# Five small bias loads on ScalarE's DMA queue, issued after adj has landed instead of at once

## What is computed

```python
def _L0_gnn_ref(x, in_mat, out_mat, w3_w, w3_b, u3_w, u3_b, w4_w, w4_b, w5_w, w5_b, u5_w, u5_b):
    h = x
    for _ in range(T):          # T = 3
        a_in = jnp.einsum('nm,bmd->bnd', in_mat, h)
        a_out = jnp.einsum('nm,bmd->bnd', out_mat, h)
        av = jnp.concatenate([a_in, a_out], axis=-1)
        z = jax.nn.sigmoid(_lin(av, w3_w, w3_b) + _lin(h, u3_w, u3_b))
        r = jax.nn.sigmoid(_lin(av, w4_w, w4_b) + _lin(h, u3_w, u3_b))
        hv = jnp.tanh(_lin(av, w5_w, w5_b) + _lin(r * h, u5_w, u5_b))
        h = (1.0 - z) * h + z * hv
    return h
...
x = _layernorm(x + _L0_gnn_ref(x, adj, adj, ...), axis=-1)
x = _layernorm(x + _L1_gnn_ref(x, adj, Wq, Wk, Wv), axis=-1)   # attention masked by adj
x = _layernorm(x + _L2_gnn_ref(x, adj, weight, bias), axis=-1) # adj @ x @ weight + bias
x = _layernorm(x + _L3_gnn_ref(x, adj, weight, bias), axis=-1) # the same with adj normalised by degree
```

## Time and profile before

| | |
|---|---|
| Median of 3 runs | 1244.99 us (1244.99 to 1246.29) |
| Profiled execution, its own time | 1243.87 us |
| Its span, first to last instruction | 1242.1 us |
| PE / PEld busy | 98% / 87% of the span |
| DVE / ACT / POOL busy | 84% / 49% / 16% of the span |
| Mean granted TensorE clock | 0.998 |

### The profile page before, as it was taken

One profiled execution on the slowest core, in us unless ns is written; L12 is line 12 of the kernel. 1 busy time (PEld: TensorE's weight loads), 2 busy tenths in 40 slices (PEclk: granted clock), 3 DMA queues, 4 the chain that ended last, 5 costly groups with the idle time before them and its releaser, 6 DMA issues.

```text
span 1242.1 us, 21043 instructions
## 1 busy us (share of the span) xinstructions
PE 1221.6 (98%) x7454; PEld 1080.8 (87%) x7454; DVE 1047.6 (84%) x2332; ACT 607.4 (49%) x1067; POOL 193.0 (16%) x334
## 2 busy tenths in 40 slices
PE   8899999999999999999999999999999999999997
PEld 7788888888988989888888888989889898898896
DVE  6679888897988979888898888979889798894899
ACT  5445545545545444544555455455454445454542
POOL 1001021020211202112020210202112020110022
PEclk9999999999999999999999999999999999999999
DMA  6021210303103031220302104031030302200001
GB/s 203 18 69 35 76 61 18 116 3 99 36 34 101 0 101 34 51 84 17 90 28 78 57 17 117 1 101 34 34 101 0 101 34 51 84 17 17 1 2 35
DMA packets 105021, 66.93 MB, mean 54 GB/s; under 512 B 65690, under 2 KB 98468, under 8 KB 104996
## 3 DMA queue, kind: packets, MB, share of 16 engines
q1 hardware_dynamic: 104784, 66.08, 17.9%
q0 software_dynamic: 192, 0.52, 0.2%
q10 hardware_dynamic: 20, 0.01, 0.0%
HBM read 35.13 MB, written 23.07 MB: 47 GB/s over the span
## 4 chain that ended last, share of the span: by engine, by line
PE 95%; DVE 3%; POOL 1%; DMA 1%; ACT 0%; issue 0%; SPq 0%; DVEq 0%; ACTq 0%
PE b_ps L489 47%; PE f_ps L489 45%; PE f_ps L615 1%; PE b_ps L662 1%; DMA b_cand<-in_L_gnn_u_w 1%; DVE f_stats L1559 0%; DVE b_stats L1559 0%; DVE b_a_lo L1605 0%; PE b_ps L519 0%; DVE normed L1579 0%; DVE f_ps L1600 0%; DVE f_rh_lo L1605 0%; POOL b_rstd L410 0%; DVE hf_feat L1579 0%; DVE result L1579 0%
## 5 line engine op out<-in xcount | busy, mean ns | idle before, releaser
L408 POOL TENSOR_TENSOR b_var_eps<-b_moments,eps 128x2 f32<-128x2 f32 x120 | 44.3, 369 | 916.5 <-DVE b_moments L1566 916.5
L1016 ACT ACTIVATE f_cand<-f_ps,bias_c 128x512 f32<-128x512 f32 x66 | 45.5, 690 | 91.2 <-PE f_ps L489 91.2
L410 POOL TENSOR_TENSOR b_rstd<-b_var_eps,neg_half 128x2 f32<-128x2 f32 x120 | 88.1, 734 | 9.4
L964 ACT ACTIVATE f_a_hi<-f_ps 128x512 fp32r<-128x512 f32 x66 | 39.5, 598 | 94.3 <-PE f_ps L489 94.2
L964 ACT ACTIVATE b_rh_hi<-b_ps 128x512 fp32r<-128x512 f32 x90 | 53.8, 598 | 64.8 <-PE b_ps L489 64.8
L1442 DVE TENSOR_TENSOR f_gate<-f_gate,hf_feat 128x512 f32<-128x512 f32 x66 | 45.5, 689 | 46.7 <-ACT f_gate L1004 46.5
L964 ACT ACTIVATE b_a_hi<-normed 128x512 fp32r<-128x512 f32 x60 | 38.0, 633 | 94.5 <-DVE normed L1579 93.1
L489 PE MATMUL f_ps<-adjT_hi,hf_node_hi 128*128 128x256 f32 x264 | 75.1, 284 | 1.1 <-DVE hb_node_lo L1495 1.1
L489 PE MATMUL f_ps<-adjT_lo,hf_node_hi 128*128 128x256 f32 x264 | 73.7, 279 | 0.0
L489 PE MATMUL f_ps<-adjT_hi,hf_node_lo 128*128 128x256 f32 x264 | 73.6, 279 | 0.0
L1004 ACT ACTIVATE f_gate<-f_ps,bias_r 128x512 f32<-128x512 f32 x66 | 45.2, 686 | 51.3 <-PE f_ps L489 51.3
(11 more groups left out here) (337 smaller groups left out, 4608.1 us busy)
## 6 DMA issues: line engine op xcount, KB each, us to landing
x_front<-in_x SPq DMA_DIRECT2D x16, 512.0 KB, 3.5
x_blocks<-in_x SPq DMA_DIRECT2D x60, 128.0 KB, 3.5
input_t<-hf_feat SPq DMA_DIRECT2D x15, 512.0 KB, 2.9
turn_sum<-normed SPq DMA_DIRECT2D x14, 512.0 KB, 2.6
result<-turn_sum SPq DMA_DIRECT2D x56, 128.0 KB, 3.0
turn_f<-f_gate SPq DMA_DIRECT2D x14, 512.0 KB, 2.7
f_z<-turn_f SPq DMA_DIRECT2D x56, 128.0 KB, 2.9
out<-result SPq DMA_DIRECT2D x14, 512.0 KB, 3.0
```

Source lines behind the costliest of these rows:

```text
L408: pool.tensor_tensor(Y.var_eps[:, g], Y.moments[:, g, :, 1], eps[:], ALU.add).then_inc(Y.s_var, 1)
L410: pool.tensor_tensor(Y.rstd[:, g], Y.var_eps[:, g], neg_half[:], ALU.pow).then_inc(Y.s_rstd, 1)
L964: return act.activation(dst, src, ACT.Copy)
L1016: act.activation(L.cand[:, k], L.ps1[:, k], ACT.Tanh, bias=bias_c[:, k:k + 1]).then_inc(L.s_tanh, 1)
```

## The change

One wait is put ahead of the five bias loads on ACT. Its semaphore is the one that the load of adj raises by 16 when it has landed.

```diff
@@ -963,6 +963,7 @@
             def copy(dst, src):
                 return act.activation(dst, src, ACT.Copy)
 
+            act.wait_ge(s_load["adj"], 16)
             for i, b in enumerate((w3_b, u3_b, w4_b, w5_b, u5_b)):
                 act.dma_start(bias_rows[C * i:C * i + C], b.rearrange("(c p) -> c p", p=P)).then_inc(s_load["bias"], 16)
```

## The result

The change made the kernel slightly slower. Its median over 20 executions is 1246.89 us (1244.63 to 1249.9), against 1245.13 us for the kernel before, timed along with it (one of its 20 executions took 2703.34 us; without it the median is 1245.05); the ratio is 1.0018, with a 95% interval from 1.0011 to 1.0024. That is 1.4 to 3.0 us. The forecast was 1245.7 with a range from 1244.2 to 1247.6, "the same" at 90%; the measured 0.18% lies just within the bound of 0.2%, and the upper end of its interval is beyond it. The profiled execution of the change took 1247.14 us, with a span of 1245.3 us and a granted clock of 0.996, where that of before had 1242.1 us and 0.998.

What follows compares the result with a forecast made beforehand. PE, busy 98% of the span, was taken as the bound. ACT 1.18 us late less a 0.48 us cushion costs PE 0.7; 1244.99 + 0.7 = 1245.7 us, range over all cases 1244.2 to 1247.6.

Steps and rivals of the forecast that it cites:

- Step 2, the price of the issues: On ACT after adj lands: the five bias issues take 1.75 us, from 3.69 to 5.44.
- q10's ring is not full: At ACT's five issues: their queue carries 20 packets against 8352 of SP's q1, so its ring is not the full one.
- Step 4, the cushion: At PE's product of adj: ACT and DVE were ready 0.48 us early, so 1.18 us late costs PE 0.7.
- the sum: Whole kernel: PE's loss of 0.7 us added to the median 1244.99 gives 1245.7 us.
- the forecast's own range: Whole kernel: 1244.3 to 1247.0 us, the sum less or plus the 1.1 to 1.3 by which runs differ.
- The rival of the clock: Opening, gap behind the u3 transposes: TensorE's clock falls, 4 us at half rate cost 2 us, 1247.8; 4%.
- late bias rows: At PE's use of the bias rows: they land at 14.6, PE stands 0.7 us more, 1246.4; 5%.
- a tail to the table load: On ACT behind the table load: a tail of some 1.4 us, PE 2.1 late, 1247.1; 3%.
- a change without effect: Opening: issues take 1.4 us, adj lands 0.3 sooner, the cushion holds ACT's 0.5 lateness, 1245.0; 8%.
- Slow issues: On ACT between 3.7 and 9: five issues held up like SP's, adjT_hi another 3.3 us late, 1249.0; 4%.

Runs made afterwards that it cites:

- table-first run: The change with a two-column copy into the existing bias_z ahead of the wait, loading the table early, no tile moved: 1244.9 us, ratio 1.0 to the kernel before.
- its second: The change once more, unedited, for a second trace, against the kernel before: 1246.84 us, ratio 1.0015.
- the filled one: The change with transposes of the identity filling PE's waits, 6 more behind those of u3, against the kernel before: 1244.98 us, ratio 1.0002.
- the filled one with the spare tile: The change with PE's waits filled by transposes and a spare 8-byte tile, against the kernel before: 1237.85 us, ratio 0.9945.
- the two filled pairs: Kernel before and change, both with PE's waits filled by transposes: 1243.48 and 1244.98 us; again with the spare 8-byte tile: 1236.64 and 1237.85 us.
- control: The kernel before, unchanged, as a run of its own, timed against the kernel before: 1245.22 us, ratio 1.0003.
- the wait for x_front: The bias loads wait for x_front instead of adj, a larger dose, against the kernel before: 1249.62 us, ratio 1.0042.
- the wait behind the issues: The wait for adj put behind the five bias issues instead of ahead of them, against the kernel before: 1245.48 us, ratio 1.0011.
- the table-first run with a tile of its own: The change with a two-column copy into a new 8-byte tile ahead of the wait, loading the table early, against the kernel before: 1237.94 us, ratio 0.9944.

## Why the prediction was right, and where it was not

**The mechanism was right.** ACT stands until adj has landed, issues five DMAs, loads its table and only then copies; the load that used to lie inside an idle time now lies on PE's path. The table-first run takes the load out of that path, keeps the late bias rows, and the cost is gone. Nothing further on gives the time back: from product start to first gate it is 10.97 us before and 11.00 after, and from there to the transposes of hb_feat 33.16 and 33.15.

**Step 2, the price of the issues, was too low.** I took 1.75 us. They took 2.02 in the profile of the change, 2.18 in its second, 2.48 in the filled one (3.56 to 6.04) and 1.74 in the filled one with the spare tile, which was also the cheaper pair. It is the third and fourth of the five that stretch, from 0.58 us together to 0.88, 1.04 and 1.24, while SP issues its own. The argument that q10's ring is not full did not exclude this. ACT's lateness at adjT_hi, forecast as 1.18, was 1.29 in the profile of the change. Over the four profiles that contain it (6.87, 7.37, 6.63, 7.12) against six without it, with or without a spare tile or the filling (5.58, 5.25, 5.57, 5.58, 5.57, 5.53), it is 1.5 us.

**Step 4, the cushion, is the one that failed.** I subtracted 0.48 us, read from one profile. It is there only when u3 lands late: of the same six profiles three have 0.5 to 0.7 us of it and three have none, 0.3 on average. In those six PE's product starts at 8.58, 7.83, 8.14, 8.81, 8.15 and 8.55, 8.34 on average, and with the change at 9.44, 9.94, 9.20 and 9.69, 9.57 on average. PE loses 1.2 us, not 0.7, and the two filled pairs measured 1.5 and 1.2 in whole executions. Of the 0.5 us that the sum missed here, 0.3 is ACT's lateness and 0.2 the cushion. (A slip beside it: the lower end of the forecast's own range, 1244.3, is 1.4 below the sum, not 1.1 to 1.3.)

**The rival of the clock was looked for in the wrong place.** I gave 4% to a fall in the opening that the change would bring about. The clock was falling already, near 53 us in the unchanged kernel. Such a fall costs 1.5 to 2.5 us: from the transposes of hb_feat to the end it is 1189.3 to 1189.5 us in the profiles without one, and 1190.9 (table first, no tile moved), 1191.7 (the change, twice) and 1191.9 (control) in those with one. In the opening it fell in three of the profiles with a late ACT and in none of those in which ACT was on time. But only two of the three had the extra gap in front of the product ahead of the fall (the wait for x_front, 3.4 us of gap, and the second one of the change, 1.8); in the wait behind the issues it had fallen by 8.0, behind the wait for u3 that the kernel before has too. And the kernel with 64 spare bytes stood 1.8 us for u3 without a fall. So the link between ACT's lateness and a fall in the opening is not shown.

A small part of the change's cost may be clock: the unfilled medians differ by 1.76 us and the ratio says 1.4 to 3.0, the filled pairs 1.2 to 1.5. 22 of 30 against 44 of 71 executions with a low mean clock is no difference that these numbers can tell from chance. The rounded mean is also a coarse mark: five of the eight executions of the change with 0.998 or more lie at 1246.2 to 1246.8, above every filled one (1245.99). By time, 25 of 30 lie above the slowest filled execution of the change, and 45 of 71 above that of the kernel before (1244.5); that leans to more falls with the change, but not clear of chance. So how much of the measured 0.18% is clock stays open.

**The rivals of late bias rows, a tail to the table load, and a change without effect** are out: the first by the table-first run, the second by every load that had work ready behind it (0.01 to 0.02 us from its end to the copy), the third by every profile of the change. Slow issues came, but mild: up to 0.7 us and not 3.3.

## What to carry to other kernels

A wait put ahead of cheap work also holds back everything behind it on that engine; look for what used to run for free in an idle time, here a table load, and ask whether it can go ahead of the wait. A cushion read as the difference between two arrivals, one of them a DMA, is a property of one execution: take it from several before subtracting it, or take it as zero. Before a difference of one or two microseconds is put down to an edit, look at the granted clock around PE's thin stretches in both kernels, and fill those stretches if the two must be compared.

## What the runs showed of the hardware that was not expected

Addresses in SBUF move the time of products: 8 unused bytes per partition ahead of the large tiles took most 128x512 products from 394 to 396 ns down to 389 to 391 and the 128x256 ones of adjT_hi with hf_node_hi from 284 to 288, and the kernel from 1244.9 to 1236.8 us; 64 bytes left the wide ones alone and made the kernel 2 us slower. A kernel that adds a small tile for another reason is therefore compared with the wrong base, as the table-first run with a tile of its own was.

The clock of one core alone goes to its lower level in the middle of a kernel that keeps PE 98% busy, in more than half of the executions. In the profile of the change it did so behind a stretch in which PE worked 1.94 of 3.5 us (50.0 to 53.5), while in that of the kernel before it stayed up behind 1.85 of 3.5, so this alone doesn't decide it. With PE's waits filled by transposes none of 32 executions has a mean clock below 0.998.

The granted clock of the windows does not show everything: it reads 1.00 over the first 5 us of the kernel before, where the weight loads of 128x128 take 231 ns. In the wait behind the issues the same kind of load takes 182 to 231 ns, 228 in the median, where 0.50 was granted (8.0 to 8.7 us), and 140 in the median where 1.00 was (5.5 to 6.2 us). Durations tell the level there, and the mean clock leaves the opening out.
